# Layer 0 of a two-layer transformer kernel: first-half q parts ahead of k's, q stack read in pieces, and some copies and squares moved between VectorE and ScalarE

## What is computed

```python
q = rms_norm(jnp.dot(x, q_kernel))        # 16 heads of 16 features, norm over all 256
k = rms_norm(jnp.dot(x, k_kernel))        # 4 key heads
v = jnp.dot(x, v_kernel)                  # 4 value heads
q = (q * qcos + rotate_half(q) * qsin)    # the same for k
logits = jnp.einsum('btkgh,bskh->bkgts', q * scale, k)
probs = softmax(logits)
encoded = jnp.einsum('bkgts,bskh->btkgh', probs, v)
x = layernorm(x + encoded.reshape(B, T, 256) @ out_kernel)
```

## Time and profile before

| | us |
|---|---|
| median of 3 runs (lowest, highest) | 892.36 (889.95, 894.5) |
| the profiled execution | 893.27 |
| its span, from the first to the last instruction | 891.2 |

### The profile page before, as it was taken

One profiled execution on the slowest core, in us unless ns is written; L12 is line 12 of the kernel. 1 busy time (PEld: TensorE's weight loads), 2 busy tenths in 40 slices (PEclk: granted clock), 3 DMA queues, 4 the chain that ended last, 5 costly groups with the idle time before them and its releaser, 6 DMA issues. The chain is left out here.

```text
span 891.2 us, 11527 instructions
## 1 busy us (share of the span) xinstructions
PE 789.9 (89%) x3907; PEld 416.9 (47%) x3908; DVE 456.1 (51%) x1213; ACT 367.1 (41%) x581; POOL 97.7 (11%) x111
## 2 busy tenths in 40 slices
PE   4599999999998989999988778878998889989886
PEld 3222434444436546666654334333464445433675
DVE  3733752563444522222256794968555755562353
ACT  3388775775761111111142205444423532157030
POOL 0000000000000011111721102231011100022000
PEclk8699999999999999999988899988999989899989
DMA  6558026015043061111117670007100450000000
GB/s 207 162 178 273 26 63 186 1 42 161 1 164 119 13 186 41 47 47 41 35 56 220 190 205 3 1 28 236 45 2 2 135 173 1 2 13 12 13 12 25
DMA packets 51582, 75.01 MB, mean 84 GB/s; under 512 B 7607, under 2 KB 44763, under 8 KB 49227
## 3 DMA queue, kind: packets, MB, share of 16 engines
q1 hardware_dynamic: 49660, 69.26, 25.8%
q0 software_dynamic: 1872, 5.11, 2.1%
HBM read 46.57 MB, written 27.66 MB: 83 GB/s over the span
## 5 line engine op out<-in xcount | busy, mean ns | idle before, releaser
L616 PE MATMUL ps<-arena 128*128 128x256 f32 (+5 forms) x1084 | 335.5, 459 | 20.1 <-DVE arena L1216 4.5
L616 PEld LDWEIGHTS ps<-arena 128*128 128x128 f32 (+1 forms) x1084 | 205.9, 200 | 113.1 <-issue 68.5
L921 ACT ACTIVATE arena<-ps 128x1024 f32<-128x1024 f32 x128 | 124.2, 1027 | 34.1 <-PE ps L650 34.0
L1016 ACT ACTIVATE arena<-ps 128x1024 f32<-128x1024 f32 (+3 forms) x128 | 83.2, 705 | 92.5 <-PE ps L854 92.3
L1382 DVE TENSOR_REDUCE arena<-ps 128x1 f32<-128x512 f32 (+3 forms) x176 | 101.2, 634 | 38.0 <-PE ps L832 37.0
L721 PE MATMUL ps<-arena 128*128 x184 | 86.6, 594 | 1.2 <-DVE arena L1287 1.2
L830 PE MATMUL ps<-arena 96*128 96x128 bf16 (+3 forms) x256 | 65.9, 314 | 14.8 <-DVE arena L1382 9.4
L650 PE MATMUL ps<-arena 96*128 96x512 bf16 x256 | 72.2, 394 | 7.2 <-DMA arena<-q_stacks_dram 4.4
L1467 POOL TENSOR_SCALAR_AFFINE_SELECT arena<-arena 128x512 f32<-128x512 f32 x64 | 42.2, 661 | 282.0 <-ACT arena L1016 281.8
L664 PE MATMUL ps<-arena 128*32 128x512 f32 x512 | 69.9, 613 | 2.9 <-DVE arena L1161 2.7
L608 PE MATMUL ps<-arena 128*128 128x128 f32 (+3 forms) x237 | 40.7, 315 | 32.6 <-DVE arena L1154 10.5
(11 more groups left out here) (145 smaller groups left out, 688.6 us busy)
## 6 DMA issues: line engine op xcount, KB each, us to landing
arena<-stacks_dram SPq DMA_DIRECT2D x16, 768.0 KB, 6.4
arena<-in_gate_up_proj SPq DMA_DIRECT2D x8, 1024.0 KB, 9.5
arena<-q_stacks_dram SPq DMA_DIRECT2D x8, 768.0 KB, 5.8
stacks_dram<-arena SPq DMA_DIRECT2D x16, 384.0 KB, 2.9
arena<-in_down_proj SPq DMA_DIRECT2D x8, 512.0 KB, 8.7
stacks_dram<-arena SPq DMA_DIRECT2D x16, 256.0 KB, 3.3
q_stacks_dram<-arena SPq DMA_DIRECT2D x8, 384.0 KB, 4.1
yg_dram<-arena SPq DMA_DIRECT2D x23, 128.0 KB, 1.7
```

The source lines that it names most:

```text
L616: last = nc.tensor.matmul(dst[0:rows, lo:hi], a, w, start=(n == 0), stop=(n == len(pairs) - 1))
L921: nc.scalar.activation(probs[:, 2 * p:2 * p + 2, :], ps[:, 2 * p:2 * p + 2, :], ACT.Exp)\
L1016: nc.scalar.activation(cprobs[:, i % 2, 2 * p:2 * p + 2, P * kt:S], ps[:, 2 * p:2 * p + 2, P * kt:S], ACT.Exp).then_inc(exp_done[p], 1)
```

## The change

- **Order of k and q.** Entry 0 of rp and T is now the first half of q, entry 1 is k, entry 2 the second half of q (`qk_columns`, `qk_width`). The factors of the norm are worked out inside rp0, after its sine and cosine products.
- **Reads of the stacks.** SP writes the parts of the first q half, then those of k; reads the first four heads of q, then k's stack, then heads 4 to 7 with a semaphore of their own, for which S b.4 waits.
- **Q.** VectorE copies the 384 columns out of PSUM. ACT squares from `qkv` in SBUF, once VectorE has copied (`consumed`), and the cosine product of rp0 waits for all the squares (`squared`).
- **T of batches 1 to 3.** VectorE makes the first part as well; ACT has no share in it any more.
- **Order strings.** Q and rp of batch 1 move from `A_START` into the first four steps of batch 0, rw moves from the first step to the fifth, and T1, T2 and X1 stand one step earlier.

```diff
-A_START = """X0 X1 Q0 Q1 Q2 Q3 rp0 rp1 +X0 +X1 V0 T0 rp2 T1 T2 +Q0 +Q1 +Q2 +Q3 +rp0 +rp1 +rp2"""
-A_FIRST = """.rw0 | | | | | +T0 .F0 | >X0 | +T1 | +T2 | .F1 | >X1 | | | .F2 | | |"""
+A_START = """X0 X1 Q0 Q1 Q2 Q3 rp0 rp1 +X0 +X1 T0 T1 V0 rp2 T2"""
+A_FIRST = """+Q0 | +Q1 | +Q2 | +Q3 +rp0 +rp1 +rp2 | .rw0 .F0 | +T0 | >X0 +T1 | +T2 | .F1 | >X1 | | | .F2 | | | |"""
...
-            return slice(C, QK0) if i == 0 else slice(P * (i - 1), P * i)
+            return slice(C, QK0) if i == 1 else slice(P * (i // 2), P * (i // 2 + 1))
...
+            def q_read(b, lo, hi, done):
+                half = lo // (NH // 2)
+                sp.dma_start(q_stack[0:STACK, b % 2, lo:hi, :],
+                             qscr[b, half].rearrange("r (d h) n -> (r d) h n", d=HD)[:, lo - NH // 2 * half:hi - NH // 2 * half, :])\
+                  .then_inc(done[b % 2], 16)
...
+                q_read(b, 0, 4, s_stack)
+                sp.wait_ge(s_scr[1], 48 * (b + 1))
                 sp.dma_start(k_stack[0:STACK, b % 2, :, :], kscr[b].rearrange("r (d h) n -> (r d) h n", d=HD))\
                   .then_inc(s_stack[b % 2], 16)
...
+                q_read(b, 4, NH // 2, s_stack1)
...
+                    if hg == 1 and kt == 0:
+                        pe.wait_ge(s_stack1[b % 2], 16 * (b // 2 + 1))
...
                         act.wait_ge(parts_ready, 3 * b)
-                        act.wait_ge(v_ready, b)
-                    src = filled(act, step)
-
-                    nc.scalar.activation(rot[:, i, 0:C], src[:, 0:C], ACT.Square, accum_out=ss[:, 0, i:i + 1])
-                    nc.scalar.activation(rot[:, i, C:QK0], src[:, C:QK0], ACT.Square, accum_out=ss[:, 1, i:i + 1])
-                    nc.scalar.activation(qkv[:, i, :], src[:, 0:QKV0], copy).then_inc(free_of(step), 1)
-                elif n == "T":
+                    consumed(act, step)
+                    if NT * b + i:
+                        act.wait_ge(squared, NT * b + i)
+                    nc.scalar.activation(resid[:, 0:C], qkv[:, i, 0:C], ACT.Square, accum_out=ss[:, 0, i:i + 1])
+                    nc.scalar.activation(resid[:, C:QK0], qkv[:, i, C:QK0], ACT.Square, accum_out=ss[:, 1, i:i + 1])\
+                      .then_inc(squared, 1)
+                elif n == "T" and b == 0:
...
+                elif n == "Q":
+                    if b and i == 0:
+                        v.wait_ge(v_ready, b)
+                    nc.vector.tensor_copy(qkv[:, i, :], filled(v, step)[:, 0:QKV0]).then_inc(free_of(step), 1)
...
+                    if i == 0:
+                        v.wait_ge(squared, NT * (b + 1))
...
+                        v.wait_ge(s_scr[i % 2], 48 * b if i == 1 else 96 * b + 24 * i)
+                        src = filled(v, step)
+                        link(nc.vector.tensor_copy(pt[:, 0, :], src[0:w, :]))
```

More of the change, by code:

```diff
@@ L367, in post_ln_layers @@
         s_stack = [sem(f"stacks_loaded{i}") for i in range(2)]
+        s_stack1 = [sem(f"second_q_stacks_loaded{i}") for i in range(2)]
         s_stack2 = [sem(f"last_q_stacks_loaded{i}") for i in range(2)]
+        squared = sem("projections_squared")
         s_full = [sem(f"scores_full{i}") for i in range(2)]
@@ L417, in qk_columns @@
         def qk_columns(i):
-            return slice(C, QK0) if i == 0 else slice(P * (i - 1), P * i)
+            return slice(C, QK0) if i == 1 else slice(P * (i // 2), P * (i // 2 + 1))
         def qk_width(i):
-            return KV0 * HD if i == 0 else P
+            return KV0 * HD if i == 1 else P
         def bank(step):
@@ L478, in layer0_parts @@
                 for j in range(3):
-                    if i == 0:
-                        dst, src = kscr[b], parts[0:w, 0, 0:3 - j, :]
+                    if i == 1:
+                        dst, src = kscr[b], parts[0:w, 1, 0:3 - j, :]
                     else:
-                        dst, src = qscr[b, i - 1], parts[0:w, i % 2, j:j + 1, :].to_broadcast([w, 3 - j, S])
+                        dst, src = qscr[b, i // 2], parts[0:w, 0, j:j + 1, :].to_broadcast([w, 3 - j, S])
                     sp.dma_start(dst[(0, 3, 5)[j]:(3, 5, 6)[j]].rearrange("r p n -> p r n"), src).then_inc(s_scr[i % 2], 16)
+            def q_read(b, lo, hi, done):
[3 more added lines that the diff above has]
+                  .then_inc(done[b % 2], 16)
             def layer0_stacks(b):
@@ L494, in layer0_stacks @@
                     sp.wait_ge(pv_done, head0 * (b - 1))
+                q_read(b, 0, 4, s_stack)
+                sp.wait_ge(s_scr[1], 48 * (b + 1))
                 sp.dma_start(k_stack[0:STACK, b % 2, :, :], kscr[b].rearrange("r (d h) n -> (r d) h n", d=HD))\
                   .then_inc(s_stack[b % 2], 16)
-                sp.wait_ge(s_scr[1], 48 * (b + 1))
-                sp.dma_start(q_stack[0:STACK, b % 2, 0:NH // 2, :], qscr[b, 0].rearrange("r (d h) n -> (r d) h n", d=HD))\
-                  .then_inc(s_stack[b % 2], 16)
+                q_read(b, 4, NH // 2, s_stack1)
                 sp.wait_ge(parts_ready, 3 * b + 3)
@@ L502, in layer0_stacks @@
                 sp.wait_ge(s_scr[0], 96 * (b + 1))
-                sp.dma_start(q_stack[0:STACK, b % 2, NH // 2:NH, :], qscr[b, 1].rearrange("r (d h) n -> (r d) h n", d=HD))\
-                  .then_inc(s_stack2[b % 2], 16)
+                q_read(b, NH // 2, NH, s_stack2)
             def gate_up_load(experts):
@@ L1133, in _ @@
                             consumed(v, ("Q", b, t))
[L1134 to L1139, removed]
                     hh2 = HD // 2
@@ L1152, in _ @@
                     link(nc.vector.tensor_tensor(flat, flat, qkv[:, :, qk_columns(i)], ALU.add))
-                    norm = rs_q[:, NT:2 * NT] if i == 0 else rs_q[:, 0:NT]
+                    if i == 0:
+                        tick(nc.vector.tensor_scalar(rs_a[:, 0:NT], ss[:, 0, :], 1.0 / C, RMS_EPS, ALU.mult, ALU.add))
+                        tick(nc.vector.tensor_scalar(rs_a[:, NT:2 * NT], ss[:, 1, :], 1.0 / (KV0 * HD), RMS_EPS, ALU.mult, ALU.add))
+                        settle()
+                        rsqrt(rs_a, rs_q, rs_b)
+                        link(nc.vector.tensor_scalar(rs_q[:, 0:NT], rs_q[:, 0:NT], 0.25, None, ALU.mult))
+                    norm = rs_q[:, NT:2 * NT] if i == 1 else rs_q[:, 0:NT]
                     nc.vector.tensor_tensor(flat, flat, norm.unsqueeze(2).to_broadcast([P, NT, qk_width(i)]),
@@ L1164, in _ @@
                     w = qk_width(i)
-                    src = bank(step)
-                    v.wait_ge(part1, 3 * b + i + 1)
+                    pt = parts[0:w, i % 2]
+                    if b == 0:
+                        src = bank(step)
+                        v.wait_ge(part1, i + 1)
+                    else:
+                        v.wait_ge(s_scr[i % 2], 48 * b if i == 1 else 96 * b + 24 * i)
+                        src = filled(v, step)
+                        link(nc.vector.tensor_copy(pt[:, 0, :], src[0:w, :]))
                     settle()
                     v.wait_ge(parts_ready, 3 * b + i)
-                    pt = parts[0:w, i % 2]
                     nc.vector.tensor_tensor(resid[0:w], src[0:w, :], pt[:, 0, :], ALU.subtract)\
```

## The result

| | before | after |
|---|---|---|
| median of 7 runs each, us | 894.0 | 901.25 |
| lowest and highest, us | 889.95, 895.45 | 899.02, 904.7 |
| profiled execution, us (its span) | 893.27 (891.2) | 901.25 (899.2) |

What follows compares the result with a forecast made beforehand. PE was taken to bound layer 0's attention, with the stack chain on the path at the start. Losses of 3.1 (batch 0, net of the earlier start), 2.8 and 0.8 sum to 6.7 us: median 899.1 us, range 893 to 905.

Steps and rivals of the forecast that it cites:

- The start: Up to the first scores of batch 0: they start at 34.4 us, 5.4 us earlier; bounds 34.0 and 36.0.
- The four Q: First steps of batch 0: batch 1's Q, moved out of the stack wait, now cost PE time; 4.1 us lost.
- VectorE's chain: Batch 0: PE's T0 and T1 of batch 1 wait for VectorE's rp and copy of rw; 4.4 us lost.
- ScalarE's new wait in batch 1: Squares of Q1 wait for VectorE's copy behind P1's norm, delaying the exp queued behind; net 2.8 us lost.
- step 4: The prediction's fourth term, ScalarE's new wait in batch 1: 2.8 us lost, 3.3 by the shared expert's work before gains.
- the two single waits: Middle of batch 1, 80 to 150 us: two PE waits set aside as ones the change leaves alone.
- Batch 2: Same wait of ScalarE for VectorE's copy of Q1 as in batch 1, a step later: 0.8 us lost.
- relief of ScalarE: Rival: batches 1 and 2 wait for exp, so work taken off ScalarE counts; some 889 or 886 us; chance 0.06.
- no change: Rival: the waits in batches 0 and 1 come out at half their size; some 895.5 us; chance 0.21.
- The low clock: Rival: batch 0 runs longer at half speed, Q of steps 1 to 3 over 2 us; 2 to 4 us, 0.12.

Runs made afterwards that it cites:

- Q in the wait: Changed kernel with Q and rp of batch 1 put back ahead of the first scores, while PE waits for the stacks; 892.03 us, ratio 0.9971 to before.
- Q on ScalarE: Changed kernel with the Q of batches 2 and 3 squared and copied out of PSUM by ScalarE alone, as before the change; 895.75 us, ratio 1.0016 to before.
- T later: Changed kernel with the three T of batch 1 each one step later and rw back in the first step; 898.57 us, ratio 1.004 to before.
- one read: Changed kernel with the first half of the q stack read in one piece of eight heads ahead of k's stack; 902.81 us in one execution.

## Why the prediction was right, and where it was off

**The start (predicted 5.4 earlier, measured 3.84).** The term was too large. Q3 was to be copied at 14.6 and was at 15.37: the sixteen matmuls of the first four Q took 7.52 us, and 6.86 in the profile of before. Among the kernels here they took 6.86 to 8.41, so I built on a short one. Another 0.43 is the read of k's stack, 4.78 us from its issue to S 0.0 where I took 4.35. The rest, some 0.35, lies in VectorE's chain and the writes between the two. The early bound of this step should have been 33.85 by its own terms (30.05 and 3.8), not 34.0.

**The four Q (predicted 4.1 lost, measured 4.05).** Right, and shown by their removal: with the Q in the wait S 0.0 to P 0.3 takes 11.71 us, 12.42 before the change, and 16.47 in the changed kernel.

**VectorE's chain (predicted 4.4 lost, measured 4.56).** Right in place and size, but made up differently. I had a wait of 2 us at T0 and one of 2 us at T1. In the profile shown T0 waited 1.87 and T1 0.51, and the lower clock took some 1.6 (0.34 in P, 0.85 in S, 0.46 in X0), so that PE came to T1 when rw was nearly copied. The clock cost nothing by P 0.6, since T1 would have waited for the copy of rw all the same. In the kernel with Q on ScalarE, with the same batch 0, the clock held behind T0 and the wait at T1 is there, in PE's timeline:

```profile
59.63 0.66 PE L615 MATMUL ps<-arena 128*128 128x128 f32 x4 [1.87 <-DVE arena L1178]
...
62.09 0.60 PE L615 MATMUL ps<-arena 128*128 128x128 f32 x4
...
64.81 1.03 PE L615 MATMUL ps<-arena 128*64 128x128 f32 x4 [2.12 <-DVE arena L1145]
```

Here the clock fell behind the wait at T1 instead, and from P 0.3 to P 1.0 it took 37.92 us against 36.87 in the changed kernel. Batch 0 as a whole came out at 4.51 later for 3.1 predicted; the short start is more than the difference.

**ScalarE's new wait in batch 1 (predicted 2.8, measured 3.47).** The exp of S 1.4 came 3.75 us later, counted from P 1.0, for 3.7 predicted, and where the clock held the wait cost 2.75, for 2.6 predicted. What I left out is the clock: S 1.5 and Q2, 1.04 and 1.46 us at full clock, took 1.95 and 2.18 behind the wait. Of these 1.63, 1.1 is lost on balance (3.85 against 2.75), as S 1.5 at full clock waits 0.31 for exp a second time. The router's copy then costs about the 0.7 that step 4 allowed: PE waits 1.21 us for ScalarE at T0, 0.63 before, and P 1.9 is 0.6 later still (so of the two single waits that I took as left alone one did grow). Against that 0.97 came back by P 1.11, where the waits for parts are gone and I had put down 0.5.

**Batch 2 (predicted 0.8, measured 0.54 by P 3.0 and 0.35 by P 3.14).** Counted from P 2.0, P 2.5 is 1.27 later than before, for 1.2 predicted, and 0.73 is given back where ScalarE no longer waits for k's parts; I had allowed 0.5 at most.

**Sum.** 6.7 predicted; P 3.14 is 8.33 later and the span 8.0 longer. By batches, batch 0 was put 1.4 too low, which is the start, batch 1 0.67 too low, and batch 2 0.45 too high. The places and waits were right; the errors of size go both ways, 2.1 too low and, with 0.33 won behind P 3.14, 0.8 too high, so luck helped by that much. The median of 901.25 is 2.15 above the forecast, but 1.64 of that is the kernel before, whose median went from 892.36 in three executions to 894.0 in seven; against that median the change costs 7.25. Not all signs came as named: P 0.3 stood at 52.41 instead of 50 to 52, T1 waited 0.51 instead of about 2, and ScalarE waited 6.15 instead of 3 to 4 ahead of the squares. What the working lacked is the clock behind a wait of PE: in batch 0 it stood in for the wait at T1, in batch 1 1.1 came on top. Of the rivals, relief of ScalarE is refuted and no change did not come. The low clock came only in part: the Q of steps 1 to 3 ran at full clock, against its sign, and the falls behind the waits cost some 1.1 us in this profile and not 2 to 4.

## What to carry to other kernels

Moving an evacuation to another engine also moves its place in a queue: here a copy that ScalarE could do at once went behind 5 us of layer norm on VectorE, and all that ScalarE does in order, exp first, waited with it. Work that fills a known wait for a DMA is free only there; ask what the same work costs where it is moved to, and whether its consumers still come late enough. When PE is the bound, cost a new PE wait at its length and allow for a lower clock behind it. Ahead of S 1.5 that added 1.1 us in one execution and nothing in another with the same wait, and behind T0 nothing, as PE had another wait ahead that took it up.

## What was not expected of the hardware

A wait of the same length did not always lower the clock: T0's 1.87 us was followed by 0.50 in the changed kernel and by 1.00 in the kernel with Q on ScalarE, where PE's next wait of 2.12 us was followed by 0.50:

```profile
59.60:62.70 3.10, 3.06 (x20) 1.39 (x20) 2.92 (x8) 0.78 (x1) 0.00 (x0) 1.00 0.00 0
...
64.80:67.60 2.80, 2.79 (x12) 0.72 (x12) 2.57 (x6) 0.00 (x0) 0.00 (x0) 0.50 0.00 0
```

PE's wait for exp at S 1.5 shows it too. It was 2.19 us in the changed kernel and 2.20 with T later, and S 1.5 took 1.95 behind it in both; it was 2.20 with Q in the wait and 2.19 with one read, and there the clock stayed at 1.00. Waits of 1.2 us for the copy of v left it at 1.00 in the changed kernel (89.3 to 92 us). With a later start, this makes the end of batch 0 vary by 2 us between executions with the same order there (P 1.0 at 89.28 to 91.27).

And the first sixteen matmuls of Q took 6.86 to 8.41 us in different executions while the clock column shows 1.00. Between 9 and 11 us five of them run in the kernel before and five in the one with Q on ScalarE; between 11 and 13 us it is eight in the first and five in the second. It reads as if PE's pace rose later in the second; the clock column does not show it, and no run here tells why.
